# An attention and MLP block on one core: the hand-written orders of all five engines are written anew

## The reference, cut to what matters

```
x = L0_attn_x                                   # 8 batches, 1024 rows, 256 features, float32
sa, ca, ga, sb, cb, gb = (silu(c) @ wmod)       # six vectors of 256 for each batch
ga, gb = sign * max(|.|, 0.25)
h = layernorm(x) * (1 + ca) + sa
scores = (h * w_lhs) @ (h * w_rhs).T            # 1024 x 1024 for each batch
x = x + ga * (softmax(scores) @ h)
h = layernorm(x) * (1 + cb) + sb
x = x + gb * (relu(h @ W1 + b1) @ W2 + b2)      # 256 -> 1024 -> 256
```

## Time and profile before

| what | value |
|---|---|
| median of 3 runs | 720.58 us (720.32 to 721.57) |
| the profiled execution | 720.58 us, of which its instructions span 718.8 us (1.8 us lie around them) |
| busy share of the span | PE 96%, PE weight loads 88%, DVE 83%, ACT 57%, POOL 49% |
| DMA | 78.59 MB, mean 109 GB/s |
| PE idle | 25.2 us of 718.8 us |
| granted TensorE clock | 0.997 of full speed (2.4 GHz) |

### The profile page before, as it was taken

How to read it: one execution, slowest core, us unless ns; L and a number is a source line. 1 busy time by engine, 2 the same in 40 slices (tenths; PEclk the granted TensorE clock), 3 DMA queues, 4 the chain that set the end, 5 groups by cost and what they waited for, 6 DMA issues and landing times.

```text
span 718.8 us, 13379 instructions
## 1 busy us (share of the span) xinstructions
...
## 2 busy tenths in 40 slices
...
DMA packets 62367, 78.59 MB, mean 109 GB/s; under 512 B 5696, under 2 KB 54912, under 8 KB 62336
## 3 DMA queue, kind: packets, MB, share of 16 engines
...
HBM read 46.68 MB, written 31.49 MB: 109 GB/s over the span
## 4 chain that ended last, share of the span: by engine, by line
PE 37%; DVE 24%; issue 10%; POOL 5%; DMA 1%; SPq 1%; DVEq 0%; POOLq 0%
PE col L557 4%; PE col L559 4%; PE col L558 4%; PE acc L500 4%; PE acc L501 4%; PE acc L506 4%; DVE Plo L811 3%; DVE Llo L893 3%; PE score L542 3%; PE score L543 3%; PE score L544 3%; DVE Rlo L895 3%; DVE score L821 2%; DVE S L787 2%; POOL ln_t L966 2%
## 5 line engine op out<-in xcount | busy, mean ns | idle before, releaser
L975 POOL TENSOR_TENSOR hid_lo<-hid,hid_hi 128x512 fp32r<-128x512 f32 x128 | 182.7, 1433 | 222.4 <-ACT hid_hi L650 222.0
L646 ACT ACTIVATE hid<-col,b1T 128x512 f32<-128x512 f32 x128 | 86.8, 678 | 118.1 <-PE col L559 113.8
L500 PE MATMUL acc<-W2hi,hid_hi 128*128 128x256 f32 x512 | 128.0, 283 | 0.0
L501 PE MATMUL acc<-W2lo,hid_hi 128*128 128x256 f32 x512 | 126.3, 280 | 0.0
L621 PE MATMUL score<-V,Phi 128*128 128x258 f32 x448 | 109.8, 281 | 0.7 <-DVE x_cur L824 0.7
L622 PE MATMUL score<-V,Phi 128*128 128x256 f32 x448 | 110.0, 283 | 0.0
L557 PE MATMUL col<-h2hi,W1hi 128*128 128x512 f32 x256 | 103.2, 403 | 1.9 <-issue 0.8
L711 ACT ACTIVATE S<-S 128x1024 f32<-128x1024 f32 x64 | 66.7, 1051 | 64.3 <-DVE S L787 49.9
L650 ACT ACTIVATE hid_hi<-hid 128x512 fp32r<-128x512 f32 x128 | 81.0, 633 | 35.4 <-PE acc L506 32.0
L559 PE MATMUL col<-h2hi,W1lo 128*128 128x512 f32 x256 | 100.7, 393 | 0.0
L558 PE MATMUL col<-h2lo,W1hi 128*128 128x512 f32 x256 | 100.3, 392 | 0.0
...
## 6 DMA issues: line engine op xcount, KB each, us to landing
block_rows<-blocks SPq DMA_DIRECT2D x30, 512.0 KB, 2.8
...
x_cur<-x SPq DMA_DIRECT2D x16, 512.0 KB, 4.2
ln_t<-x SPq DMA_DIRECT2D x14, 512.0 KB, 6.5
score_blocks<-stage SPq DMA_DIRECT2D x14, 512.0 KB, 3.5
...
out<-x_mlp SPq DMA_DIRECT2D x8, 512.0 KB, 3.7
...
```

The costliest lines, as they stand in the source:

```text
L500: nc.tensor.matmul(o, hi, W2hi[:, it, :], start=(it == 0 and t % 2 == 0), stop=False, skip_group_check=True)
L501: nc.tensor.matmul(o, hi, W2lo[:, it, :], start=False, stop=False, skip_group_check=True)
L646: nc.scalar.activation(hid[:, n % 2, :], col[n % 2][:], ACT.Relu, bias=b1T[:, n % FT:n % FT + 1]).then_inc(col_read, 1)
L975: G.tensor_tensor(hid_lo[:, n % RING, :], hid[:, n % 2, :], hid_hi[:, n % RING, :].bitcast(F32), ALU.subtract).then_inc(hid_lo_done, 1)
```

## The change

The tables are replaced. No step is added or removed, no instruction changes, the semaphores stay. Of the body of the loop (STEPS), the lines for PE, DVE and SP:

```diff
     "pe": """
-        SC.0 F.0- SC.1 SC.2 F.1- SC.3 F.2- F.3- F.4- SC.4 G.0- MB.0 G.1- SC.5 G.2- F.5- SC.6 G.3- SC.7 F.6-
-        F.7- G.4- F.8- G.5- AV.0 G.6- G.7- MB.1 F.9- F.10- AV.1 G.8- AV.2 F.11- F.12- AV.3 G.9- F.13- G.10-
-        AV.4 G.11- F.14- AV.5 F.15- AV.6 G.12- AV.7 G.13- G.14- G.15-
+        F.0- SC.0 SC.1 SC.2 F.1- SC.3 SC.4 F.2- MB.0 G.0- SC.5 F.3- SC.6 SC.7 F.4- G.1- G.2- F.5- F.6- G.3-
+        G.4- F.7- G.5- F.8- F.9- G.6- AV.0 G.7- MB.1 F.10- F.11- F.12- AV.1 G.8- AV.2 G.9- G.10- F.13- AV.3
+        G.11- AV.4 F.14- F.15- AV.5 G.12- G.13- G.14- AV.6 AV.7 G.15-
     "dve": """
-        SC.0 B2.1- ST.0 SC.1 XG.2- ST.1 XG.3- VL.0 L1.0+ SC.2 V.0 SC.3 ST.2 ST.3 BH.0+ SC.4 SB.0 SC.5 T2.1-
-        VL.1 SB.1 SC.6 V.1 L1.1+ SM.0 SB.2 SB.3 SC.7 MX.0 SM.1 OUT.0- AV.0 SM.2 SB.4 BH.1+ AV.1 SM.3 SB.5
-        AV.2 SM.4 TH.0+ AV.3 SM.5 SB.6 AV.4 B2.0 SB.7 XG.0 SM.6 XG.1 AV.5 SM.7 TH.1+ AV.6 T2.0 AV.7 OUT.1-
+        SC.0 SC.1 XG.2- B2.1- SC.2 XG.3- ST.0 SC.3 VL.0 ST.1 ST.2 SC.4 L1.0+ SC.5 ST.3 V.0 SC.6 SC.7 BH.0+
+        SB.0 SB.1 VL.1 SB.2 SB.3 T2.1- V.1 MX.0 SM.0 SM.1 L1.1+ OUT.0- SB.4 SB.5 SB.6 AV.0 SM.2 AV.1 BH.1+
+        AV.2 SM.3 XG.0 SM.4 SM.5 AV.3 TH.0+ SB.7 B2.0 XG.1 SM.6 AV.4 AV.5 TH.1+ SM.7 AV.6 T2.0 AV.7 OUT.1-
     "sp": """
-        AM.0 GA.0- S2.1- XT.0+ R2.1- SW.0 X1.0 SR.0 SW.1 SH.0+ GB.0 XT.1+ SR.1 RH.0+ SH.1+ O0.0- RH.1+ S2.0
-        R2.0 O1.0- O1.1- X0.0+
+        AM.0 GA.0- S2.1- X1.0 XT.0+ SW.0 R2.1- SR.0 SW.1 SR.1 SH.0+ XT.1+ RH.0+ GB.0 SH.1+ O0.0- RH.1+ S2.0
+        R2.0 X0.0+ O1.0- O1.1-
```

In batch 0 (FIRST_STEPS), DVE's list from AV.3 on, ACT's second half and one place of PE:

```diff
-    dve ... AV.2 AV.3 SB.6 SB.7 B2.0 AV.4 TH.1+ XG.0 AV.5 XG.1 AV.6 T2.0 AV.7 VO.0
+    dve ... AV.2 AV.3 XG.0 SB.5 SB.6 B2.0 SB.7 XG.1 AV.4 TH.1+ AV.5 AV.6 T2.0 AV.7 VO.0
-    act ... EX.2 EX.3 EX.4 EX.5 TH.1+ EX.6 EX.7 T2.0
+    act ... EX.2 EX.3 EX.4 TH.1+ EX.5 EX.6 EX.7 MC.0 T2.0
```

In batch 1 (SECOND_STEPS) PE's MB.1 moves up to stand between F.7 and G.5, and MX stands earlier on DVE:

```diff
-    pe  ... F.7- G.4- G.5- F.8- MB.1 G.6- AV.0 ...  AV.5 AV.6 AV.7 G.14- G.15-
+    pe  ... F.7- MB.1 G.5- F.8- G.6- AV.0 G.7- ...  G.13- AV.6 G.14- G.15- AV.7
-    dve XG.2- VL.0 SC.0 ... SB.1 L1.1+ SB.2 MX.0 V.1 SM.0 SM.1 SB.3 SB.4 ...
+    dve VL.0 XG.2- SC.0 ... T2.1- BH.0+ SC.7 MX.0 V.1 SM.0 L1.1+ SB.3 SB.4 ...
```

More of the change, by code:

```diff
@@ L30 @@
     "pe": """
-        MA.0+ T0.0+ MF.0+ MF.1+ T0.1+ SA.0+
+        MA.0+ T0.0+ MF.1+ MF.0+ T0.1+ SA.0+
     """,
@@ L49 @@
     "pe": """
-        MF.2 SC.0 MF.3 SC.1 SC.2 MD.0 SC.3 SC.4 SC.5 SC.6 SC.7 MB.0 MB.1 AV.0 AV.1 AV.2 AV.3 AV.4 AV.5 AV.6
-        AV.7 WR.0
+        SC.0 MF.2 MF.3 SC.1 SC.2 MD.0 SC.3 SC.4 SC.5 SC.6 SC.7 MB.0 MB.1 AV.0 AV.1 AV.2 AV.3 WR.0 AV.4 AV.5
+        AV.6 AV.7
     """,
     "act": """
-        WS.0 MC.0 EX.0 EX.1 L1.0+ TH.0+ EX.2 EX.3 EX.4 EX.5 TH.1+ EX.6 EX.7 T2.0
+        WS.0 L1.0+ EX.0 EX.1 TH.0+ EX.2 EX.3 EX.4 TH.1+ EX.5 EX.6 EX.7 MC.0 T2.0
     """,
     "dve": """
-        L1.0+ SC.0 MF.0 SC.1 GA.0 SC.2 BH.0+ SC.3 SC.4 SC.5 SC.6 SC.7 SB.0 SB.1 SB.2 SB.3 L1.1+ SB.4 SB.5
-        AV.0 BH.1+ AV.1 TH.0+ AV.2 AV.3 SB.6 SB.7 B2.0 AV.4 TH.1+ XG.0 AV.5 XG.1 AV.6 T2.0 AV.7 VO.0
+        SC.0 MF.0 L1.0+ SC.1 GA.0 SC.2 BH.0+ SC.3 SC.4 SC.5 SC.6 SC.7 SB.0 SB.1 L1.1+ SB.2 SB.3 AV.0 BH.1+
+        SB.4 AV.1 TH.0+ AV.2 AV.3 XG.0 SB.5 SB.6 B2.0 SB.7 XG.1 AV.4 TH.1+ AV.5 AV.6 T2.0 AV.7 VO.0
     """,
     "pool": """
-        L1.0+ N1.0+ XC.0 WS.0 L1.1+ N1.1+ XC.1 XC.2 L2.0 N2.0 XC.3 L2.1
+        L1.0+ N1.0+ WS.0 XC.0 XC.1 L1.1+ N1.1+ XC.2 XC.3 L2.0 N2.0 L2.1
     """,
     "sp": """
-        AM.0 GB.0 SH.0+ XT.1+ RH.0+ SH.1+ RH.1+ S2.0 R2.0 X0.0+
+        GB.0 AM.0 SH.0+ XT.1+ RH.0+ SH.1+ RH.1+ S2.0 X0.0+ R2.0
     """,
@@ L74 @@
+        G.10- F.13- F.14- G.11- F.15- G.12- G.13- AV.6 G.14- G.15- AV.7
     """,
     "act": """
-        F.0- V.0 F.1- L1.0+ F.2- T2.1- EX.0 F.3- SM.0 F.4- F.5- MC.0 EX.1 F.6- V.1 SM.1 TH.0+ F.7- EX.2 SM.2
-        F.8- EX.3 EX.4 F.9- F.10- SM.3 SM.4 F.11- EX.5 SM.5 F.12- EX.6 TH.1+ F.13- F.14- SM.6 EX.7 SM.7
-        F.15- T2.0
+        F.0- V.0 F.1- F.2- F.3- T2.1- EX.0 EX.1 F.4- EX.2 F.5- V.1 F.6- SM.0 L1.0+ SM.1 F.7- EX.3 SM.2 F.8-
+        SM.3 F.9- EX.4 TH.0+ F.10- SM.4 EX.5 F.11- SM.5 MC.0 F.12- TH.1+ EX.6 F.13- F.14- SM.6 EX.7 F.15-
@@ L91 @@
-        O0.0- X0.0+ O1.0- O1.1-
+        AM.0 GA.0- S2.1- XT.0+ SW.0 X1.0 R2.1- SR.0 SW.1 SR.1 SH.0+ XT.1+ RH.0+ SH.1+ GB.0 O0.0- RH.1+ S2.0
+        R2.0 O1.0- O1.1- X0.0+
     """,
```

55 lines of the change are left out of this document (27 added, 28 removed).

## The result

The changed kernel takes 728.18 us, median of 4 runs (727.42 to 729.83), beside 721.08 us (720.32 to 722.79) for the kernel before on the same chip. The ratio is 1.0098, with a 95% interval of 1.007 to 1.0126: slower by 1.0%. The prediction said 714.6 us and faster. The profiled execution took 729.4 us, its instructions span 727.6 us.

The account below looks back on a forecast made before the run. A pass was PE's 83.0 us of work plus 2.0 of wait for DVE, the bound at its end. From 718.8: +0.9 batch 0, -2.8 batch 1, -3.7 loop, -0.4 batch 7, +1.8 around the span: 714.6 us, range 708.5 to 721.5.

Parts of the forecast that it names:

- F.0 ahead of SC.0: PE, end of a pass: cover for AV.7's add falls to 2.8 us; F.0 can't start before DVE begins AV.7.
- DVE's queue: DVE from AV.3 to AV.7 in a pass: 21.6 us where SM.6 misses POOL, giving F.0 a wait of 0.3.
- XG.0 behind O0: DVE in each pass: XG.0 waits about 1.2 us for O0's landing; costs 0.1, or 1.1 if SM.2 met POOL.
- Collisions: DVE and POOL in the loop: 1.0 us for each meeting; three meetings taken, 1.0 on the path.
- ln_t later: XT.0's load in the loop goes out later; PE waits 0 to 0.4 us in SC.6, taken as 0.
- The first batch: Batch 0: AV.5 and AV.6 start later, F.0 moves from 75.65 to about 76.5; cost 0.9 us.
- The second batch: Batch 1: PE's idle before MB.1 and in AV.6 both go; 83.9 us, a gain of 2.8.
- The last batch and behind: Batch 7 gains 0.4 us with the step to the next phase; AFTER_STEPS and the tail change by 0.
- DVE's margin of 1.1 at AV.3: DVE in a pass: without XG.0's wait it reaches AV.3 about 1.1 us ahead of PE.
- slower, through ln_t: Rival, chance 0.15: ln_t lands late, PE stands inside SC.6, losing up to 2.3 us a pass; above 721 to 726.
- The wait stays and changes its name: Rival, chance 0.15: PE waits 2 us at F.0 for T2.0, passes stay at 85.0; time 719.6 us.
- The sentence on the Trainium skill: DVE with two SBUF inputs and POOL exclude each other; XG.0 may lose a whole L975, a pass 1.1 us longer.

Follow-up runs that it names:

- XG.0 back: The changed kernel with DVE's XG.0 in the loop moved from before SM.4 to behind SB.7, ahead of B2.0: 720.92 us, 0.9983 of the kernel before.
- O0 earlier: The changed kernel with SP's store O0 in the loop issued ahead of GB.0 and SH.1: 722.67 us, 1.0007 of the kernel before.
- XC earlier: The changed kernel with POOL's XC.1 and XC.2 ahead of L1.1 in the loop, XC.3 behind F.10: 720.28 us, 0.9972 of the kernel before.
- all three: The changed kernel with XG.0 behind SB.7, MB.1 ahead of AV.0, SB.4 ahead of OUT.0 and POOL's XC steps earlier: 721.15 us, 0.9997.
- B2.0 later: The changed kernel with DVE's XG.1 and SM.6 ahead of B2.0 in the loop: 723.65 us, 1.0039 of the kernel before.
- best_b: The changed kernel with all loop repairs, old tables for batch 0 and the final MLP, and batch 1's MB.1 behind F.8: 714.95 us, 0.9912.
- before, F.0 first: The kernel before with one step moved, PE's loop beginning F.0 SC.0 and not SC.0 F.0: 716.0 us, 0.9928 of the kernel before.

## Why the prediction was wrong, point by point

The third pass of the changed kernel and of seven others gives this table. "Late" is the start of DVE's AV.3 less the end of PE's AV.3; "queue" is DVE's time from AV.3 to AV.7; "PE" is the time from PE's end of AV.3 to its next F.0. All are read off the start times of steps in the timelines.

| kernel | late | queue | PE | PE's own work | pass |
|---|---|---|---|---|---|
| changed | 2.21 | 22.12 | 24.56 | 21.3 | 86.2 |
| XG.0 back | 0.20 | 22.64 | 23.07 | 21.3 | 84.8 |
| O0 earlier | 0.79 | 22.12 | 23.14 | 21.3 | 84.8 |
| XC earlier | 0.61 | 22.10 | 22.94 | 21.3 | 84.4 |
| all three | 0.20 | 22.62 | 23.05 | 21.3 | 84.5 |
| B2.0 later | 2.09 | 20.99 | 23.31 | 21.3 | 85.0 |
| best_b | 0.20 | 21.62 | 22.04 | 21.3 | 83.5 |
| before, F.0 first | 2.76 | 22.67 | 25.66 | 25.5 | 83.8 |

In every row PE's time is late + queue + 0.23, and in the rows of the new table the pass is PE's 82.9 and what PE's time has over its own work, within 0.2. So F.0 starts when DVE gets to AV.7, and in the new table nothing else sets the pass. PE's own work between is four AV, five G and two F in the new table (21.3, as the prediction had it) and four AV, seven G and three F in the old (25.5). The prediction had the 21.3 but never held it against the old table's 25.5: the new table has 4.2 us less of PE's work behind AV.3, so it needs DVE on time there, and the old one can bear a lateness of about 2.6 (25.5 less its queue of 22.67 and the 0.23).

The step that failed is the lateness of DVE at AV.3, for which the sum had 0.6 us and the runs show 2.21 (points 3 and 4); the queue behind it was also taken 0.5 too short (point 2).

Point by point:

1. *F.0 ahead of SC.0.* Right: worth 1.2 us a pass in either table, and F.0 waits for T2.0 as said.
2. *DVE's queue.* Taken at 21.6, measured 22.12. TH.0 and TH.1 met POOL neither time (2.7 each), but SM.6 did (2.32): by the parts that is 22.7 - 2.0 = 20.7. B2.0's idle, called "filled" and set to 0, was 1.58, more than the 0.84 of the earlier trace rows, and this makes it 22.2. L2.0 on POOL waits for the statistics of AV.3, so N2.0 slipped with AV.3. Between AV.3 and B2.0 stand TH.0 and SB.7 now, 3.9 us, where SM.5, SB.6 and AV.4 had stood, 4.3; and from DVE's start of AV.3 to B2.0 it is 7.3 us (399.84 to 407.17) and was 7.0 (393.23 to 400.24). The prediction counted what came in ahead of B2.0 and not what went out. A wait on another engine's answer moves along with what triggers it.
3. *XG.0 behind O0.* The wait was foreseen at 1.2 and was 1.25. Its cost was taken at 0.1 in one case and 1.1 in the other, and the sum took neither: it had 0.6 for this and the collisions together.
4. *Collisions.* Foreseen for SM.2 at 1.0; it cost 1.9, since it lost to two POOL steps, F.10 and XC.3. But that two stood back to back isn't enough for this: the row from which the 1.0 was taken is SM.2 too, and there POOL also had two in a row, but DVE got in between them and the second one was held up (3.54 us for the two, 1.29 for one alone). There SM.2 began 0.14 us into the first step, in the changed kernel 0.53. The prediction priced the meeting and not the moment at which it happens. Three collisions were taken; two came, SM.2 and SM.6, both on the path. Here the sum failed. DVE's margin of 1.1 at AV.3 fits: SM.2's 1.9 and XG.0's 1.25, less 1.1, and the 0.2 by which DVE starts an AV behind PE at best, are the 2.2 of the table. The same sum gives 1.0 with O0 earlier and 0.5 with XC earlier, where the table has 0.79 and 0.61. With SM.2 in the way both costs come in full behind the margin, and the sum held 0.6 for the two together. It had also left out the 0.23 from DVE's start of AV.7 to F.0, and dropped the 0.3 of part 2 by which DVE begins behind PE: with it the wait at a queue of 21.6 is 0.6, not 0.3. Lateness 1.6, queue 0.5, this 0.2, and 0.1 of rounding the other way: 2.2 us a pass, from 84.0 to 86.2. Over five passes that is some 11 us of the 14.8 by which the profiled execution (729.4) missed the 714.6; points 6 to 8 are the rest.
5. *ln_t later.* Right at 0. The load is now issued at 348.55 and lands at 353.24, before DVE gets to it; the page has its median at 4.7 us, where the earlier trace rows had 6.5 (the prediction's 6.58 is 6.60 by the two times beside it):

```profile
ln_t<-x SPq DMA_DIRECT2D x14, 512.0 KB, 4.7
```

6. *The first batch.* Predicted 0.9 later, measured 2.7. The waits that were named are 1.2 of it (from AV.1 to F.0 28.81 us before, 29.96 now). Another 1.3 is the clock during AV.0, in matmuls that the change doesn't touch: AV.0 took 5.04 us in the kernel before and 6.35 here. The windows, of before and then of after:

```profile
42.00:48.00 6.00, 6.00 (x22) 5.02 (x23) 6.00 (x13) 5.90 (x9) 3.98 (x6) 0.77 0.01 3
```

```profile
42.00:48.00 6.00, 5.97 (x15) 4.80 (x16) 3.90 (x11) 5.88 (x8) 3.77 (x8) 0.53 0.02 3
```

 The same table gave 0.72 with O0 earlier, 0.50 with XG.0 back and 1.00 with B2.0 later, where AV.0 took 3.58 us and the first batch ended at 75.93. So this is a spread from run to run and no effect of the tables.

7. *The second batch.* Predicted 2.8 shorter, measured 1.3. The idle in AV.6 went, that before MB.1 stayed at 2.1, for the same DVE step as in the earlier trace rows, because DVE stood for a load that the count of its steps had left out. PE, then DVE:

```profile
113.73 0.62 PE L605 MATMUL score<-ident,row_max 128*128 128x128 f32 x4 [2.08 <-DVE row_max L803]
...
107.02 0.69 DVE L792 TENSOR_TENSOR S<-lower,score 128x512 f32<-128x512 f32 x1 [2.60 <-DMA lower<-score_blocks]
```

 PE stood 2.08 us; DVE had stood 2.60 us, until 107.02, for the transposed scores (SR.1), whose load SP issued at 101.95, against 99.01 in the kernel before.
8. *The last batch and behind.* Taken at -0.4 and 0, measured +0.1 and +0.3, the latter a wait of F.7 for ACT (L646, 0.8) that was not named.

Of the rivals, "slower, through ln_t" named the wrong mechanism. "The wait stays and changes its name" was the right one: XG.0 waits, SM.2 and SM.6 collide, F.0 stands for T2.0. It was priced at 85.0 a pass with 2 us of wait at F.0; PE lost 3.3 (24.56 less 21.3), of which 0.6 + 1.3 + 0.7 stand as idle in its timeline. Its conditions were right and its price wasn't worked out: it took the old wait over instead of putting its own delays through the sum of part 2.

The sentence on the Trainium skill (SBUF — State Buffer, on its two sides) was about XG.0, which met no POOL step in the passes. The same section of the Trainium skill says that the one that starts first holds the shared ports for its whole instruction, and the trace agrees for SM.2 in that it ended behind both POOL steps. By that rule SM.2 would lose what was left of F.10 when it began (387.18 less 386.42, 0.8 us), by the nearest row 1.0. It lost 1.9, the whole of XC.3 as well, so at this place the sum would have been no nearer by the rule; the measurement decides.

Of the signs that were named, the passes at 83.5 to 84.5 us and the end of L605's wait for L803 didn't come. The waits of L557 for L898 and of L938 for the DMA came, at the size foreseen, and so did one of the signs for "wrong": PE idle for Plo, 6.5 us in all.
